# A transformer layer in split f32r: where xh, xl and the stage buffers stand in SBUF

## What is computed

```
x = x + attention(layernorm(x))     # qkv = n @ qkvw + qkvb; softmax(q k^T / sqrt(32)) v; @ ow + ob
x = x + (silu(n @ W_gate.T) * (n @ W_up.T)) @ W_down.T      # n = layernorm(x)
```

## Time and profile before

| | us |
|---|---|
| median of 3 runs | 3513.61 |
| the profiled execution | 3510.52 |
| its span, first to last instruction | 3508.6 |
| PE busy | 3311.1 |
| DVE busy | 2069.4 |
| ACT busy | 1453.7 |
| POOL busy | 808.5 |

### The profile page before, as it was taken

One profiled execution on the slowest core, in us unless ns is written; L12 is line 12 of the kernel. 1 busy time (PEld: TensorE's weight loads), 2 busy tenths in 40 slices (PEclk: granted clock), 3 DMA queues, 4 the chain that ended last, 5 costly groups with the idle time before them and its releaser, 6 DMA issues.

```text
span 3508.6 us, 40890 instructions
## 1 busy us (share of the span) xinstructions
PE 3311.1 (94%) x15264; PEld 2552.3 (73%) x15264; DVE 2069.4 (59%) x3236; ACT 1453.7 (41%) x2702; POOL 808.5 (23%) x600
## 2 busy tenths in 40 slices
PE   6999999987989999999998999999879899999999
PEld 5676777654778888888676767677548788888885
DVE  5688888889552332332458888888894423223222
ACT  1478777777321111111015787777772211111110
POOL 1133333236400110110102333332463011010110
PEclk9999999998999999999789999999999999999996
DMA  3423343344311111111224233333443111111111
GB/s 105 122 76 95 87 106 87 87 119 125 133 43 54 54 36 53 55 37 37 99 78 112 76 109 82 92 91 87 119 133 112 43 60 48 36 60 48 37 45 48
DMA packets 110518, 274.62 MB, mean 78 GB/s; under 512 B 28720, under 2 KB 29872, under 8 KB 106224
## 3 DMA queue, kind: packets, MB, share of 16 engines
q1 hardware_dynamic: 110320, 272.02, 26.3%
HBM read 195.37 MB, written 76.02 MB: 77 GB/s over the span
## 4 chain that ended last, share of the span: by engine, by line
PE 73%; DVE 15%; DMA 4%; SPq 3%; ACT 2%; issue 1%; POOL 1%; POOLq 0%; ACTq 0%; DVEq 0%
PE ps L522 12%; PE ps L524 12%; PE ps L523 12%; PE ps L677 6%; PE ps L679 5%; PE ps L678 5%; PE ps L587 5%; PE ps L623 4%; PE ps L606 4%; PE ps L618 4%; DVE mx L890 4%; DVE pl L914 4%; SPq L1053 3%; DVE wl L848 2%; DMA wraw<-in_wqkv 1%
## 5 line engine op out<-in xcount | busy, mean ns | idle before, releaser
L890 DVE TENSOR_REDUCE mx<-ps 128x1 f32<-128x512 f32 x1024 | 696.0, 686 | 128.9 <-PE ps L587 117.3
L735 ACT ACTIVATE pu<-ps 128x512 f32<-128x512 f32 x1024 | 620.0, 605 | 346.3 <-PE ps L606 341.6
L1012 POOL TENSOR_TENSOR pl<-pu,ph 128x512 fp32r<-128x512 f32 x320 | 435.4, 1361 | 922.2 <-ACT ph L736 922.1
L736 ACT ACTIVATE ph<-ps 128x512 fp32r<-128x512 f32 x1024 | 620.0, 605 | 0.0
L914 DVE TENSOR_TENSOR pl<-pu,ph 128x512 fp32r<-128x512 f32 x704 | 550.3, 783 | 65.3 <-ACT ph L736 61.8
L522 PE MATMUL ps<-xh,gh 128*128 128x512 f32 x1376 | 546.0, 397 | 14.0 <-DVE gl L959 7.4
L524 PE MATMUL ps<-xl,gh 128*128 128x512 f32 x1376 | 541.9, 394 | 0.0
L523 PE MATMUL ps<-xh,gl 128*128 128x512 f32 x1376 | 538.1, 391 | 0.0
L587 PE MATMUL ps<-kst,qst 96*128 96x512 f32 x1024 | 432.4, 422 | 78.9 <-DVE mx L890 54.3
L968 DVE TENSOR_TENSOR hf<-ps,sg 128x512 f32<-128x512 f32 (+1 forms) x88 | 60.9, 692 | 721.4 <-PE ps L524 703.5
L606 PE MATMUL ps<-qst,kst 98*128 98x512 f32 x1024 | 421.6, 412 | 5.8 <-ACT ph L736 5.3
(11 more groups left out here) (83 smaller groups left out, 4981.8 us busy)
## 6 DMA issues: line engine op xcount, KB each, us to landing
wraw<-in_wqkv SPq DMA_DIRECT2D x24, 1024.0 KB, 5.0
q_d<-stg SPq DMA_DIRECT2D x384, 64.0 KB, 1.7
k_d<-stg SPq DMA_DIRECT2D x384, 64.0 KB, 1.7
qst<-q_d SPq DMA_DIRECT2D x64, 384.0 KB, 3.8
kst<-k_d SPq DMA_DIRECT2D x64, 384.0 KB, 4.6
graw<-in_wg SPq DMA_DIRECT2D x44, 512.0 KB, 4.5
graw<-in_wu SPq DMA_DIRECT2D x42, 512.0 KB, 3.6
draw<-in_wd SPq DMA_DIRECT2D x42, 512.0 KB, 3.7
```

The costliest lines, as they stand in the source:

```text
L735: e.activation(pu[sl][:, :], bk[:, :], ACT.Exp, scale=SCALE).then_inc(s["a_p"], 1)
L736: e.activation(ph[sl][:, :], bk[:, :], ACT.Exp, scale=SCALE).then_inc(s["a_ph"], 1)
L890: e.reduce_max(mx[:, (b * HEADS + j) % 2, t, half:half + 1], ps[2 + bank_of[what, b, j, t, half]][:, :], AX.X).then_inc(s["v_mx"], 1)
```

## The change

xh and xl are allocated ahead of the small tensors, behind a pad that is computed from the base and 1024, and the zone's start is rounded up to a multiple of 128 instead of 32. No instruction is added, removed or moved.

```diff
         def sb(name, shape, dt=f32):
             return ctx.enter_context(nc.sbuf_tensor(name, shape, dt))
 
+        pad = -nc.sbuf_base % 1024
+        if pad:
+            sb("pad", [P, pad // 4])
+        xh = sb("xh", [P, KT, S], f32r)
+        xl = sb("xl", [P, KT, S], f32r)
         idt = sb("idt", [P, P])
         bqk_c = sb("bqk_c", [P, 2 * KT])
         bv_b = sb("bv_b", [P, H])
         mv = sb("mv", [P, TT, 2])
         st6 = sb("st6", [P, TT, 12])
         rs = sb("rs", [P, 5, TT])
-        xh = sb("xh", [P, KT, S], f32r)
-        xl = sb("xl", [P, KT, S], f32r)
         mx = sb("mx", [P, 2, TT, 2])
         mm = sb("mm", [P, 2, TT])
         zt = [sb(f"zt{i}", [P, HD]) for i in range(2)]
-        zone = -(-nc.sbuf_base // 32) * 32
+        zone = -(-nc.sbuf_base // 128) * 128
```

## The result

The changed kernel takes 3542.5 us (median of 4 runs, 3540.4 to 3545.3) against 3516.1 us before (3511.6 to 3524.0, the same number): a ratio of 1.0073, 95% interval [1.0052, 1.0095]. It is slower, by some 26 us, where no difference was forecast, and it lies 10 us above the range. (The median of the kernel before was 3512.6, 3513.7 and 3513.3 us beside the later experiments, 63 runs in all; against those the loss is 29 us.) The lines of the code moved down by three: L522 to L524 are now L525 to L527, L587 is L590, L641 to L643 are L644 to L646, L677 to L679 are L680 to L682.

What follows compares the result with a forecast made beforehand. PE was taken to bound both feed-forward and attention. All terms were 0 on the profiled 3510.5 us; with the median of the runs 3.1 us higher, the forecast was 3513 us, no difference that can be told (0.50), range 3452 to 3532.

Steps and rivals of the forecast that it cites:

- What bounds the kernel: Whole kernel: PE bounds feed-forward and attention, busy 3311 of 3508.6 us; wrong if its busy time shifts over 7 us.
- Addresses: SBUF layout: xh starts at 17440, not a multiple of 1024; xh and xl keep their phase, the zone moves to 88704.
- Parts (2) and (3), the moving operand: Matmuls streaming xh/xl (5664) or zone buffers (6208 and 3072): 0 us; bound for the zone streams 98 us gain.
- rival A: Matmuls streaming now-aligned zone buffers lose the extra sixteenth per step: 3412 us, or 3438 with a fixed part; chance 0.15.
- Part (4), the zone buffers as weights: Weight loads from gh, gl, wh, wl, qst, hh, hl: 0 us taken; gate/up bounded at -9 to +17 us.
- Rival C: Gate/up locks in its slow step as xh and gh lose their common phase modulo 64: 17 us, 3527; chance 0.21.
- Rival B: Matmul time above the 17/16 floor goes, the sixteenth stays: 57 us, 3454, or a third of it, 3492; chance 0.14.
- Parts (5) and (6): DVE, ACT and POOL on zone buffers, and DMAs into the zone: 0 us each; bounds 5 and 12 us either way.

Runs made afterwards that it cites:

- e3: Changed kernel with the pad computed from the rounded base, xh at 17408 and zone at 88704: 3525.8 us, ratio 1.0038 to the kernel before.
- e8: Changed kernel's order without a pad, xh at 16512 and zone at 87872, distance 192 as in the kernel before: 3513.8 us, one run.
- e2: Changed kernel's order and pad, but the zone at 88800, 96 modulo 128 as in the kernel before: 3513.3 us, ratio 0.9999.
- e5: Kernel before with the zone 256 bytes later and gh and gl alone 192 bytes lower, gate/up distance 0 modulo 256: 3505.7 us, ratio 0.9976.
- e6: Kernel before with the zone 256 bytes later and gh and gl alone 96 bytes lower, gate/up distance 96 modulo 256: 3536.2 us, ratio 1.0061.

## Why the prediction was wrong

- **What bounds the kernel**: held. PE, by its steps, took nearly the whole loss; its busy time grew by 33.8 us, where the prediction called itself wrong from 7 on.
- **Addresses**: held. xh stood at 17440, 32 above a multiple of 1024, and no alignment of its own would have helped (e3, e8).
- **Parts (2) and (3), the moving operand**: the zero was right. The down-projection keeps 226.8 ns at 0 modulo 128, so rival A and its estimated 75 to 98 us are refuted. The transposes, which I had read as weak evidence for alignment, are none: eight of them take 1.03 us after idt lost its place at 0 modulo 128, and took 1.04 before.
- **Part (4), the zone buffers as weights: the step that failed.** I took 0 "since the same addresses show either step in the output projection" and concluded that "the surcharge follows the history of the queue more than the address". One address does show both 113.3 and 117.8 ns (the kernel before goes from one to the other in the middle of its first batch, e2 has 113.3 in both batches, e8 first 117.8 and then 113.3); what chooses was not found, and that it is history is not shown. But the distance of the two operands sets which steps there are to choose from, and at the changed kernel's distances the fast ones are gone: gate/up went from 229.2 to 234.2 ns, V from 116.4 to 119.8, output projection from 116.9 to 120.1, q and k from 231.4 to 233.2. Having seen two steps at one address, I took the address for unimportant, where two steps at one address say nothing about another address. The bound of +17 us for gate/up was near its 20.6; V and output projection had no bound of their own on this side.
- **Rival C**: the right place and sign, with its cause half right. I asked for a common phase modulo 64; the period is 256 (e3 has a common phase modulo 128 and is slow, at 233.2 ns). The sign it would show by, gate/up at 231 ns or more with the down-projection unchanged, is what came. Its price of 17 us left out V, output projection and q/k, 12.9 us in the profiled pair, and rated gate/up at the slowest step seen before (233.2) where 234.2 came. That put the range's end at 3532, and 3542.5 came.
- **Rival B**: its argument (the down-projection, in phase, runs at the floor) was right for gate/up, and e5 collects 8 us of the 9.5 priced. Of the other 48 us next to nothing was had by placement: q and k fell by 1.7 ns at distance 0, the context matmuls (232.6 to 233.2 ns everywhere) answer to nothing tried, and L606 is at 233.7 ns at best. (Its full price is 3454 where it is worked out and 3452 where the range begins; the 2 us change nothing.)
- **Parts (5) and (6)**: held. DVE's busy time changed by 1.7 us and POOL's by 2.2; PE waits 12.2 us for kst, 12.4 before.

## What to carry to other kernels

When matmuls stream f32r operands back to back with a weight load each, measure the step from start to start in each stage, and look at the distance between the two tensors modulo 256 bytes, not at their alignment; place each stage's weights against its own moving operand, since here the best distance was another for streams of 512 columns (gate/up) than for those of 256 (output projection, V). A stage with two steps at one address isn't independent of the address. And look at the granted clock and at the steps where the last tile of a dimension is short: filling it up with zeros to full height was worth 49 us here, where the best placement was worth 8.

## What the runs showed of the hardware

- With distance 0 gate/up, a stream of 512 columns, steps at 226.7 ns, at both absolute places tried; at 32 to 160 and 224 at 233 to 234 ns; at 192 at 229. For the 256 columns of the output projection the order is another: at 0 the step is 120.0 ns, at 64 and at 192 it is 113.3 or 117.8. The floor of the down-projection, seventeen sixteenths of the clean time or 226.7 ns, stays in all 14 kernels; the output projection reaches the same share, 113.3 ns, only at distances 64 and 192. What makes the sixteenth stays open; alignment doesn't.
- The step of a stream therefore depends on where its weights stand, by up to 7.5 ns in 227. The Trainium skill ("TensorE: Matmul & The Clock Gate", Step-by-step) says that loading the next tile's weights takes no read bandwidth from the running matmul, since PE has two independent read ports; e6, where only the weights' place was changed and gate/up went from 229.2 to 234.2 ns, doesn't fit with that. That both reads meet in parts of SBUF that repeat every 256 bytes is my reading of the table, and not shown apart from it.
- 96 matmuls of which half have 64 rows held the clock at its lower level for 51 to 61 us with PE busy without a break, in the first batch of all 13 profiled kernels that have them and in the second of 11; the same 96 with the 64-row ones at 128 rows, half of those rows zero in one operand, left it up for the most part (mean 0.84 and 0.94 in those stretches). In the profiled runs of e3 and e6 the second batch escaped the fall without any such change, and they are 15 and 23 us below their kernels' medians.
- At the upper clock a change between 64 and 128 rows makes two steps of 0.32 to 0.34 us where 0.227 is the rule (e6 and e3, second batch: 30.7 us for the 96).
